# Routing stage in another order: gate logits from attention output and normalised x, ranking in the next step, first slots loaded under fewer conditions

## What is computed

```python
def conv(x, Wq, bq, Wk, bk, Wv, bv, Wr, br):      # q, k, v: 64 channels each
    q, k, v = x @ Wq + bq, x @ Wk + bk, x @ Wv + bv
    maps, vectors = softmax(k, over tokens of the image), softmax(v, over tokens of the image)
    desc = einsum('bnd,bnv->bvd', q, maps)
    return einsum('bvd,bnv->bnd', desc, vectors) @ Wr + br

def ffn(x, Wg, W1, W2, W3, b3):                   # 8 experts, F = 384, top 2
    logits = x @ Wg
    top_logits, top_idx = top_k(logits, 2)
    weight = softmax(top_logits)                  # of the two
    act = silu(x @ W1[e]) * (x @ W3[e] + b3[e])
    return sum over the two experts e of weight_e * act @ W2[e]

x = x + conv(layernorm(x, eps=1e-6), ...)
out = x + ffn(layernorm(x, eps=1e-5), ...)
```

## Time and profile before

| | |
|---|---|
| median of the runs | 361.66 us |
| profiled execution, own time | 359.97 us |
| its span | 358.2 us |
| PE, DVE, ACT, POOL busy | 272.7, 238.3, 182.7, 171.8 us |
| mean granted TensorE clock | 0.883 |
| HBM read and written | 17.51 and 12.01 MB |
| chain that ended last, by engine | PE 38%, issue 13%, DVE 11%, POOL 7%, DMA 5% |

### The profile page before, as it was taken

One profiled execution on the slowest core, in us unless ns is written; L12 is line 12 of the kernel. 1 busy time (PEld: TensorE's weight loads), 2 busy tenths in 40 slices (PEclk: granted clock), 3 DMA queues, 4 the chain that ended last, 5 costly groups with the idle time before them and its releaser, 6 DMA issues.

```text
span 358.2 us, 7758 instructions
## 1 busy us (share of the span) xinstructions
PE 272.7 (76%) x1723; PEld 219.2 (61%) x1724; DVE 238.3 (67%) x811; ACT 182.7 (51%) x464; POOL 171.8 (48%) x221
## 2 busy tenths in 40 slices
PE   1988886838296858444499999998999999999500
PEld 0445553515173534311499989998999899989400
DVE  4357886475667637450288878887888788878824
ACT  3446572516173342300167767776777677767300
POOL 4000064707074664771026656665666567656710
PEclk9999998969588965558599999999999999999955
DMA  3998001101010100121222222222222222117059
GB/s 110 343 273 269 21 30 32 52 7 52 7 44 24 55 30 31 53 74 46 54 67 76 62 60 55 66 62 62 58 60 59 59 58 58 54 59 235 31 171 312
DMA packets 31819, 29.83 MB, mean 83 GB/s; under 512 B 4993, under 2 KB 29505, under 8 KB 31665
## 3 DMA queue, kind: packets, MB, share of 16 engines
q1 hardware_dynamic: 24704, 18.38, 18.1%
q0 software_dynamic: 4320, 8.92, 7.6%
q10 hardware_dynamic: 2768, 2.23, 1.9%
HBM read 17.51 MB, written 12.01 MB: 82 GB/s over the span
## 4 chain that ended last, share of the span: by engine, by line
PE 38%; issue 13%; DVE 11%; POOL 7%; DMA 5%; another core or an unknown queue 4%; SPq 3%; ACT 2%; DVEq 1%; POOLq 0%; ACTq 0%
PE bank L674 7%; PE bank L656 6%; PE bank L657 6%; PE bank L658 6%; PE bank L664 5%; POOL result_rows L1213 4%; PE bank L676 3%; DMA w_all<-result_rows 3%; PE bank L644 2%; POOL w_all L1208 2%; SPq L444 1%; PE bank L590 1%; SPq L443 1%; PE bank L550 1%
## 5 line engine op out<-in xcount | busy, mean ns | idle before, releaser
L1189 POOL DMA_INDIRECT sorted_rows<-row_buf,position x64 | 64.8, 1012 | 93.3 <-issue 51.4
L1213 POOL DMA_INDIRECT result_rows<-w_all,xs x71 | 70.9, 999 | 21.1 <-issue 19.9
L590 PE MATMUL bank<-all_ones 128*128 128x512 bf16 x205 | 67.1, 441 | 13.5 <-DMA bkv<-L_conv_bv_dram 7.6
L674 PE MATMUL bank<-w_down,act_hi 128*128 x213 | 59.0, 345 | 1.5 <-ACT y_parts L845 0.8
L1208 POOL TENSOR_TENSOR w_all<-y_parts 128x128 f32<-128x128 f32 x71 | 32.5, 457 | 54.7 <-ACT y_parts L845 53.6
L656 PE MATMUL bank<-w_up,xs_hi 128*128 x142 | 54.9, 386 | 0.0
L1112 DVE TENSOR_TENSOR w_all<-bank,b_all 128x384 f32<-128x384 f32 x71 | 39.5, 557 | 23.0 <-PE bank L658 22.7
L840 ACT ACTIVATE act_hi<-bank 128x384 fp32r<-128x384 f32 x71 | 34.9, 491 | 29.4 <-issue 15.8
L657 PE MATMUL bank<-w_up,xs_lo 128*128 x142 | 48.7, 343 | 0.0
L658 PE MATMUL bank<-w_up,xs_hi 128*128 x142 | 48.5, 342 | 0.0
L676 PE MATMUL bank<-w_down,act_lo 128*128 x213 | 47.6, 224 | 0.0
(11 more groups left out here) (137 smaller groups left out, 431.6 us busy)
## 6 DMA issues: line engine op xcount, KB each, us to landing
xs<-sorted_rows SPq DMA_DIRECT2D x71, 65.0 KB, 1.8
w_all<-result_rows SPq DMA_DIRECT2D x16, 256.0 KB, 4.1
w_all<-L_ffn_W_dram SPq DMA_DIRECT2D x2, 1536.0 KB, 8.7
x_all<-x_dram SPq DMA_DIRECT2D x8, 256.0 KB, 4.3
out_dram<-w_all ACTq DMA_DIRECT2D x8, 256.0 KB, 4.0
w_all<-L_ffn_W_dram SPq DMA_DIRECT2D x3, 512.0 KB, 11.3
b_all<-L_ffn_b_dram SPq DMA_DIRECT2D x1, 1536.0 KB, 9.3
result_rows<-w_all,xs POOLq DMA_INDIRECT x71, 2.3
```

What stands on the lines that cost most here:

```text
L590: nc.tensor.matmul(bank[free_bank][:].rearrange("p (a b) -> p a b", a=4), all_ones[:], all_ones[:].unsqueeze(1).broadcast_to([P, 4, P]), s ...
L674: nc.tensor.matmul(bank[7][:, 0:2 * C], act_hi[s.par][:, k * P:(k + 1) * P], w, start=(k == 0), stop=False)
L1189: nc.gpsimd.indirect_dma_start(out=sorted_rows.ap(), out_offset=bass.IndirectOffsetOnAxis(ap=position[u.par][:, c:c + 1], axis=0), in_=row ...
L1213: nc.gpsimd.indirect_dma_start(out=result_rows.ap(), out_offset=bass.IndirectOffsetOnAxis(ap=xs[s.ring][:].bitcast(I32)[:, DEST:DEST + 1], ...
```

## The change

- Gate logits: the gate uses the layer norm of x1 = x + attention output. Its two best experts do not depend on the positive factor 1/std, nor on the mean if the columns of Wg are centred (`wg_mid`). So the logits up to this factor are x1 @ wg_mid. The attention part comes out of `attend` itself, because Wr, br and all made from them get 8 more columns (CE = C + E = 136), Wr @ wg_mid and br @ wg_mid. The part of x is `logits_of_x` (normalised x, transposed, which is there for keys and values, times wg_mid), scaled back by `std_x`. `transpose_tn`, `copy_tnt` and `route` are gone; the gap of the two logits is scaled by 1/std of x1 one step later (`scale_gap`).
- br is added in PSUM by two small matmuls (`spread_br`) instead of `add_br` on DVE.
- `choose` (now `choose_pair` and `choose_experts`) moves to the step of the unit's `attend`; `rank`, `weigh_and_place` and the scatter to the next step (before: two steps later on PE and POOL).
- `normalise_probs` goes from DVE to ACT; the maximum takes one operation less.
- The first three experts are loaded ahead of x of units 4 to 7, the others behind it. POOL rounds and splits these three before its first scatter; ACT and DVE do the other five, in steps 0 to 4 and 1 to 5.
- The fillers in the steps are gone, except 8 in each of steps -1 and 0 and 10 ahead; the 24 ahead of the slots no longer wait for the tables. All steps are written out instead of looped, from -3 to 9.
- The last unit but one is counted too. A slot of expert 0 that is full by then (`rows_needed`, slots 0 to 7) waits on `scattered[1]` for three of the four odd batches only. The 8 paddings are shared by SP and ACT.
- `down` makes its three products of the high half first and waits for the low half only after them.

```diff
+            load_experts_of(0, LOADED_FIRST, early_in)
+            for u in range(4, NU):
+                load_x(Step(0, u))
+            load_experts_of(LOADED_FIRST, E, late_in)
...
-            for e in range(E):
-                n_rows = sp.value_load(count_i[0:1, e:e + 1], min_val=0, max_val=TOK)
-                sp.dma_start(sorted_rows[ds(n_rows + e * REGION, P), :], pad_rows[:, e, :]).then_inc(pads_in, 16)
+            for e in range(0, E, 2):
+                pad_region(sp, e)
...
                     sp.wait_ge(pads_in, 16 * (E + SPARE))
-                    for i in range(2):
-                        sp.wait_ge(scattered[i], 16 * SCATTERS * (NU // 2))
+                    sp.wait_ge(scattered[0], 16 * SCATTERS * (NU // 2))
+                if isinstance(s, int) and s < FILLED_FIRST:
+
+                    rows = sp.value_load(rows_needed[0:1, s:s + 1], min_val=ROWS_FILLED, max_val=ROWS_ALL)
+                    wait_in_front(sp, waited_sp, (scattered[1], rows))
+                elif isinstance(s, int) and s == FILLED_FIRST:
+                    sp.wait_ge(scattered[1], ROWS_ALL)
...
+            def logits_of_x(u):
+
+                at_least(pe, x_logits_sb, u.n)
                 for t in range(TPU):
-                    last = nc.tensor.matmul(bank[6][:, t * E:(t + 1) * E], tn_t[:, t * P:(t + 1) * P], wg[:],
+                    last = nc.tensor.matmul(bank[6][:, t * E:(t + 1) * E], xn_t[:, t * P:(t + 1) * P], wg_mid[:],
                                             start=True, stop=True)
```

More of the change, by code:

```diff
@@ L340, in exists, with has_norms @@
         def exists(u):
[L342 removed]
+            return 0 <= u.n < NU
+        def has_norms(m):
+            return 0 <= m.n < NU + 3
         def mean_var_read(n):
@@ L733, in exp_kv, with normalise_probs @@
                 last.then_inc(exp_done, 1)
+            def normalise_probs(u):
+                act.wait_ge(inv_ready, u.n + 1)
+                at_least(act, attn_ps, u.n - 1)
+                for m in range(2):
+                    last = nc.scalar.activation(probs[u.par][:, m, :], exps[:, m, :], ACT.Copy,
+                                                scale=inv_sum[:, m:m + 1])
+                last.then_inc(probs_ready, 1)
             def copy_pk(u):
@@ L794, in iteration @@
                     copy_pk(i)
-                if exists(i.shift(-2)):
-                    exp_gap(i.shift(-2))
+                if has_norms(later):
+                    rough_rstd(later)
                 if exists(old):
-                    normalise_t(old)
+                    exp_gap(old)
+                if i.n == -1:
+                    copy_logits_of_weights()
+                    round_br()
                 if exists(i):
@@ L801, in iteration @@
                 if exists(old):
-                    normalise_tiles(old, [TPU - 1])
-                first = isinstance(i.n, int) and i.n == -1
-                if first:
-                    normalise_x(i.shift(2))
-                    copy_products()
+                    normalise_t(old)
+                if exists(later):
+                    normalise_x(later)
+                if i.n == -2:
+                    copy_wq()
+                    copy_wr_t()
                 if exists(new):
                     exp_kv(new)
-                if exists(old):
-                    copy_tnt(old)
-                if exists(i.shift(2)) and not first:
-                    normalise_x(i.shift(2))
-                if exists(i):
-                    round_weights(i)
-                if not isinstance(i.n, int) or i.n < NU:
-                    rough_rstd(i.shift(3))
-            rough_rstd(Step(0, 0))
-            run_units(act, iteration)
-            exp_gap(Step(0, NU - 1))
+                    normalise_probs(new)
+                if i.n == -1:
+                    copy_products()
+                if 0 <= i.n < E - EARLY:
+                    round_weights(i.shift(EARLY))
+            run_units(iteration)
+            act.wait_ge(count_ready, 1)
+            for e in range(1, E, 2):
+                pad_region(act, e)
             act.wait_ge(rows_ready, NU)
@@ L961, in normalise_probs @@
-            def normalise_probs(u):
-                dve.wait_ge(exp_done, u.n + 1)
-                after(nc.vector.reciprocal(inv_sum[:], exp_sum[:]), sum_steps, u.n + 1)
-                at_least(dve, attn_ps, u.n - 1)
-                for m in range(2):
-                    last = nc.vector.tensor_scalar(probs[u.par][:, m, :], exps[:, m, :], inv_sum[:, m:m + 1], None, ALU.mult)
-                last.then_inc(probs_ready, 1)
+                after(nc.vector.tensor_reduce(neg_max[:], bank[1][:].rearrange("p (m n) -> p m n", m=2), AX.X,
+                                              ALU.max, negate=True), max_steps, u.n + 1)
@@ new lines, in add_x, with scale_x_logits, add_logits @@
+                last.then_inc(x1_ready, 1)
+            def scale_x_logits(u):
+                dve.wait_ge(x_logits_ps, u.n + 1)
+                nc.vector.tensor_tensor(x_logits[u.par][:],
+                                        bank[6][:, 0:TPU * E].rearrange("p (t e) -> p t e", e=E),
+                                        std_x[u.par][:].unsqueeze(2).broadcast_to([P, TPU, E]),
+                                        ALU.mult).then_inc(x_logits_sb, 1)
+            def add_logits(u):
+                dve.wait_ge(attn_ps, u.n + 1)
+                dve.wait_ge(x_logits_sb, u.n + 1)
+                for m in range(2):
+                    last = nc.vector.tensor_tensor(
+                        logits[:, 2 * m:2 * m + 2, :],
+                        bank[4 + m][:, 0:2 * CE].rearrange("p (s c) -> p s c", s=2)[:, :, C:CE],
+                        x_logits[u.par][:, 2 * m:2 * m + 2, :], ALU.add)
+                after(last, logits_steps, u.n + 1)
```

418 lines of the change are left out of this document (253 added, 165 removed).

## The result

| | before | changed |
|---|---|---|
| median of the runs | 361.58 us (360.61 to 361.95, 4 runs) | 345.97 us (344.70 to 346.72, 4 runs) |
| profiled execution, own time and span | 359.97 and 358.2 us | 345.99 and 344.2 us |
| PE, DVE, ACT, POOL busy | 272.7, 238.3, 182.7, 171.8 us | 255.7, 233.2, 184.4, 182.1 us |

The account below looks back on a forecast made before the run. PE was taken to bound the slots, so only routing and the gap could give much: 10.0 from placing the last unit earlier plus 9.9 from the gap, 19.9 less, 361.66 to 341.8 us; range 329 to 357 for 8 in 10.

Parts of the forecast that it names:

- the case called the forecast: Whole kernel: the case that the forecast itself holds, a time of 336 to 347 us; chance 0.42.
- Start: Before the routing steps: waiting for late weights until 32.3 us puts the end of step 0's `add_eps` effectively at 34.4, 3.1 later.
- T0: The moment when `add_eps` ends in a routing step, on which the next step's DVE and ACT work hangs.
- One step: One routing step, counted from the end of `add_eps`: 12.95 us at full clock and 14.4 at half.
- Seven steps: Routing: 95.2 us at full clock or 105.3 at half, splits included; 103 taken, with PE's signals assumed in time.
- late signals as a rival: Routing: PE's signals late in one or two steps, +6.8 us each, giving 348.6 to 355.4 us; chance 0.22.
- The last unit: End of routing: the last unit is placed in step 8, at 141.3 us against 151.3, saving 10.0.
- The gap: Between routing and slots: pads on two queues, bounds 7.4 and 15.4 us, 10.5 taken against 20.4, saving 9.9.
- First slots ahead of the last scatters: Slots 0 to 6 wait for fewer scatters: gives nothing if the pads come last, up to 3 us if not.
- Slots: Slot stage with `down` doing hi products first: PE is full, so 0 us, at best -1.5.
- Clock: PE's clock in routing without fillers: three quarters at half speed, mostly 0.5; range term -8 to +2 us.
- The number of instructions: From a batch's start to the end of `attend`: about 70 instructions afterwards; fewer was a weak sign of timely signals.

## Why the prediction was right, and where its terms were off

The forecast was 341.8 us in a range of 329 to 357; the result, 345.97, lies inside, and inside that of the case called the forecast (336 to 347). Its parts, in order:

- *Start.* ACT waits for the late weights until 32.39 (32.3 forecast), but only for 0.49 us, and T0 is 35.5 in place of 34.4. The chain that ended last in this stretch does not run through that wait but through the four instructions of `find_shift` beside POOL's splits, 4.7 us longer than elsewhere. The forecast's sum held nothing for such a loss: it came, and hid almost whole. Up to 1.1 us of it may have reached T0; the other path (ACT's weights, TensorE's 8 fillers, the copy of `pk` that ends at 35.54) ends at the same moment. One of the forecast's signs of being wrong, DVE's instructions growing beside POOL's, did show, at this small cost. POOL's splits: 11.9 us for three experts (bounds 8.2 to 24.7), so free at 29.5, nearer to the early bound of 25, and no scatter was late.
- *One step.* Right where nothing is late. From T0 = 63.76 in the run without scatters, `add_logits` starts at T0+9.56 (9.5 forecast at half clock), and from there to the end of `add_eps` it is 4.55 (4.9). A full step is 14.1 us. The split's +0.9 was wrong: it lies in the wait for TensorE and costs nothing. The first and the last step are shorter (12.3 and 11.2), which the sum did not have.
- *Seven steps.* 103 forecast, 104.6 measured, and right for the wrong reason. It is two errors that cancel: clean steps at half clock take 94.0, not 105.3, and late signals add 10.6, for which the term held nothing. "I take that they do [come in time]" is the sentence that failed, and with it "no `remote` wait of DVE": the forecast had late signals as a rival that costs 6.8 us in single steps. They cost 1.7 to 3.3 us in each of four steps and next to nothing in the others, and lie between DVE's own instructions, since `attend` now escapes them. The removal of fillers was argued as their cure; the run of before without fillers shows that it shortens them (5.82 to 2.44 us) and does not end them. Of the 11.3 us by which 105.3 is too long, 4.5 are the splits, 4.7 the short first and last step, and 2.1 a full step of 14.1 in place of 14.4.
- *The last unit.* T0+3.9 forecast, T0+3.6 measured. Placed at 143.6 in place of 141.3.
- *The gap.* The term that was mis-sized: 15.8 us against 10.5 taken, just above the upper bound of 15.4. The bound had assumed three slow intervals of before (12.0); they took 11.5. What it left out is that slot 0 now reads `rows_needed` after the wait for the pads: from the end of that wait to the load are 0.8 us, at instructions of normal length. I had put the slow stretch at a fixed time after the batches' start; by the runs it lies where the scatters lie. On a chip without it the gap is 8.4 (lower bound 7.4).
- *First slots ahead of the last scatters.* "Gives nothing if the pads come last": they did, and undoing it changes nothing measurable.
- *Slots.* Taken 0 with a best of -1.5, measured -2.0, and the order of the down products is the cause of some 1.7 to 2.0. The +3 of the range stood for a cost of the weight loads, which no run shows; a slot became shorter (2.196 to 2.198 us in place of 2.234 to 2.235).
- *Clock.* Half in nearly all of routing, as forecast (a granted clock of 0.56, 0.50 and 0.50 in 50 to 80, 80 to 110 and 110 to 130 us). The three quarters at half in the sum were the author's estimate; no row showed such a share. The fillers do go with shorter products in the kernel before: 0.59 to 0.70 us with them in its first five units and 1.06 or more in its last three, 1.06 or more in all eight without. The row of the granted clock, which reads 1.00 in just the run without, does not speak against it, since that trace has no record of the clock there.
- *The number of instructions.* The prediction took the counts of instructions in four windows (73 and 89 with the signal in time, 86 and 94 with it late) for a weak sign that fewer of them help. The shorter waits without fillers (2.44 us in place of 5.82) would agree; but no run shows more of it: the kernel with plain writes has as many instructions (7287 against 7292) and more packets (39793 against 31904), and no late signal.

So the change gains 15.6 us as 7.7 in routing (10.2 from the last unit's step and 1.7 in the others, less the 4.2 by which the start is later), 4.7 in the gap, 2.0 in the slots, and the rest between one profiled execution and the medians. Of these only the slots' part was undone in a run of its own (undoing the early slot loads changed nothing); that the gap's comes from pads on two queues is read from the traces. By the estimate for the undisturbed chip, some 6 to 10 of the 15.6 are there only because less lies in the scatters' way.

## What to carry to other kernels

Before costing a step, ask of each delay in the old trace whether it is the program's or a neighbour's: a delay that ends near the last indirect scatter of a batch may be the scatter's, and an edit can move it rather than end it. Queue instructions beside scatters are dear where this happens: four pads took 11.8 us there, 3.7 in the run without scatters, and 1.8 with half the instructions and the scatters put behind them. But what then lies beside the scatters pays; here it was the slot loads, and the time hardly moved. Before reading a clock row, look whether the trace has a record of the clock there, and check it with a product of known length. Put one control of the kernel before and one of the changed kernel into each set of runs, since here the same kernel took 338 us in one place and 362 in another, and the gain was not the same share in both.

## What the runs showed of the hardware that was not expected

- In two sets of runs of three, and in that of the result, GpSimd's indirect scatters delay other engines. VectorE's own successive instructions wait 1.0 and 1.99 us for each other, `add_x` of the kernel before starts 6.5 us after `attend` has ended (66.38 and 72.92), and instructions of SP's queue take 0.70 us in place of 0.02 to 0.3. In the third set, on another chip, with the same scatters, nothing is delayed: `mean_var` waits 0.18 us for `stats`, and SP's assert takes 0.02.
- Beside a split of GpSimd (1.80 or 0.98 us), a VectorE instruction with two inputs in SBUF lasts until the split ends: 1.70, 0.92, 1.72 and 1.03 us in place of 0.16. Instructions with one input, or with one of two in PSUM, keep their length (`stats` 0.86 us, `mix` 0.45).
- A window of the granted clock reads 1.00 ahead of the trace's first record: products of 1.06 us stand there. In all traces, where there are records, the product of 512 columns takes 0.59 to 0.70 us at 1.00 and 1.06 to 1.22 at 0.50.
- Fillers ahead of waiting products cost the kernel before 4.5 us while they shortened its products (0.70 us in place of 1.13 at the median for the one of 512 columns).
- GpSimd rounds 128x768 elements in 0.82 us and splits them in 1.80; DVE's split takes 0.96.
